# Candidate sums of a two-layer bidirectional GRU kept in the accumulator bank, with zeroings and output sigmoids in another place

## What is computed

```python
def step(hprev, gxt):
    gh = hprev @ whh.T + bhh
    r = jax.nn.sigmoid(gxt[:, :h] + gh[:, :h])
    z = jax.nn.sigmoid(gxt[:, h:2 * h] + gh[:, h:2 * h])
    n = jnp.tanh(gxt[:, 2 * h:] + r * gh[:, 2 * h:])
    hn = (1.0 - z) * n + z * hprev
    return (hn, hn)
...
fwd = _bigru(x_inner, ...)
bwd = jnp.flip(_bigru(jnp.flip(x_inner, 1), ...), 1)
y = jax.nn.silu(fwd + bwd) * jax.nn.silu(z)
```

## Time and profile before

| | |
|---|---|
| median of three runs | 1040.92 us |
| the profiled execution | 1043.19 us, its span 1041.2 us |
| the two loops (L2, L3) | 387.5 us each, 775 us of the span |
| busy in the span | PE 937.9 us (90%), DVE 831.3 (80%), ACT 746.7 (72%) |

### The profile page before, as it was taken

How to read it: one execution, slowest core, us unless ns; L and a number is a source line. 1 busy time by engine, 2 the same in 40 slices (tenths; PEclk the granted TensorE clock), 3 DMA queues, 4 the chain that set the end, 5 groups by cost and what they waited for, 6 DMA issues and landing times. The chain is left out here.

```text
span 1041.2 us, 54627 instructions
## 1 busy us (share of the span) xinstructions
PE 937.9 (90%) x22226; PEld 839.5 (81%) x22226; DVE 831.3 (80%) x4987; ACT 746.7 (72%) x4622; POOL 47.3 (5%) x24
## 2 busy tenths in 40 slices
PE   5678797799999999999999879999999999999997
PEld 3644785488988888888888747989888988888886
DVE  7753348688888888999999776888888899999993
ACT  4424571688888888888888528888887888888882
POOL 2001241100000000000000030000000000000000
PEclk9587899755555555555555557555555555555555
DMA  5020500000000000000000000000000000000001
GB/s 144 3 26 5 141 14 6 1 5 4 4 4 4 4 5 4 4 4 4 4 4 4 3 6 3 4 4 4 4 4 4 4 4 5 4 5 4 4 4 31
DMA packets 15000, 13.07 MB, mean 13 GB/s; under 512 B 12372, under 2 KB 13909, under 8 KB 14461
## 3 DMA queue, kind: packets, MB, share of 16 engines
q1 hardware_dynamic: 14749, 9.58, 3.8%
HBM read 8.74 MB, written 0.83 MB: 9 GB/s over the span
## 5 line engine op out<-in xcount | busy, mean ns | idle before, releaser
L1285 PE MATMUL L3s_cand_sum<-L_states,L_w_hidden 97*128 97x8 bf16 x2048 | 171.2, 174 | 0.0
L1285 PE MATMUL L2s_cand_sum<-L_states,L_w_hidden 97*128 97x8 bf16 x2048 | 171.2, 174 | 0.0
L1285 PE MATMUL L2s_reset_sum<-L_states,L_w_hidden 97*128 97x8 bf16 x2048 | 142.1, 180 | 2.5 <-DVE L_states L1147 1.7
L1285 PE MATMUL L3s_reset_sum<-L_states,L_w_hidden 97*128 97x8 bf16 x2048 | 142.1, 180 | 2.4 <-DVE L_states L1147 1.7
L1147 DVE TENSOR_TENSOR_SCAN L_states<-L3s_renew,L3s_terms 96x32 f32<-96x32 f32 x512 | 113.0, 221 | 23.0
L1147 DVE TENSOR_TENSOR_SCAN L_states<-L2s_renew,L2s_terms 96x32 f32<-96x32 f32 x512 | 113.0, 221 | 23.0
L1285 PE MATMUL L3s_keep_sum<-L_states,L_w_hidden 97*128 97x8 bf16 x2048 | 130.0, 174 | 0.0
L1285 PE MATMUL L2s_keep_sum<-L_states,L_w_hidden 97*128 97x8 bf16 x2048 | 130.0, 174 | 0.0
L1285 PEld LDWEIGHTS L3s_cand_sum<-L_states,L_w_hidden 97*128 97x128 f16 x2048 | 128.5, 104 | 0.0
L1285 PEld LDWEIGHTS L2s_cand_sum<-L_states,L_w_hidden 97*128 97x128 f16 x2048 | 128.4, 104 | 0.0
L1285 PEld LDWEIGHTS L2s_reset_sum<-L_states,L_w_hidden 97*128 97x128 f16 x2048 | 105.6, 112 | 21.8 <-issue 2.2
(11 more groups left out here) (252 smaller groups left out, 3160.1 us busy)
## 6 DMA issues: line engine op xcount, KB each, us to landing
L_wih_raw<-in_L_wih SPq DMA_DIRECT2D x2, 1152.0 KB, 11.1
lagged<-in_L_w SPq DMA_DIRECT2D x1, 1296.0 KB, 8.4
L_w_hidden_raw<-in_L_whh SPq DMA_DIRECT2D x2, 576.0 KB
stream<-in_x SPq DMA_DIRECT2D x2, 384.0 KB, 3.8
out<-stream SPq DMA_DIRECT2D x4, 192.0 KB, 2.1
l_idft<-in_idft SPq DMA_DIRECT2D x1, 400.0 KB
rpe_lw<-in_rpe_lw SPq DMA_DIRECT2D x1, 384.0 KB
lagged<-coefs SPq DMA_DIRECT2D x16, 24.0 KB, 2.2
```

What stands on the lines that cost most here:

```text
L1285: return e.matmul(dst, weights.hidden[0:rows, wp, GATES * (2 * g + j) + gate, :], rhs, start=False, stop=False, skip_group_check=True)
```

## The change

Three things. First, `candidate` no longer writes an SBUF tile: the scan writes into the third or fourth quarter (by q's parity) of the same candidate bank whose first two quarters it reads, and the tanh reads it there. Second, every zeroing and every output sigmoid on ScalarE now stands directly behind a reset sigmoid, through a new function `between`: a group's reset half behind its own reset sigmoid at s = 0, the other group's keep half behind the reset sigmoid at s = 1. Before, group 0's zeroings and all output sigmoids stood behind the tanh, and group 1's zeroings behind group 0's reset sigmoid of the step after. Third, TensorE's waits follow: the wait for the zeroed keep half moves to the hidden keep products, a step earlier in the count for group 1, and group 0's six keep input products are shared over five steps (s = 3 to 7) in place of six.

```diff
-        cand = pairs("cand", [C, 2, PER, 2])
...
+        cand = lambda g, q: cand_bank[g][q // STEPS % 2][0:C, 2 + q % 2].rearrange("p c s -> p (c s)")[:, 0:2 * PER]
...
-                    e.tensor_tensor_scan(flat(cand[g][:, x]), flat(reset[g][:, x]), flat(cand_sum(g, p)[0:C, :, :, s]), 0.0,
+                    e.tensor_tensor_scan(cand(g, q), flat(reset[g][:, x]), flat(cand_sum(g, p)[0:C, :, :, s]), 0.0,
                                          ALU.mult, ALU.add).then_inc(cand_ready[g], 1)
...
-                def zero(g, q):
-                    p, s = q // STEPS % 2, q % STEPS
-                    if 1 <= q // STEPS < CHUNK_COUNT - 1:
+                def zero(g, q, sums):
+
+                    e.activation(sums(g, 1 - q // STEPS % 2)[0:C], zeros[:], ACT.Copy).then_inc(zeroed[g], 1)
+
+                def between(g, q):
+
+                    chunk, s = divmod(q, STEPS)
+                    if 1 <= chunk < CHUNK_COUNT - 1:
                         if s == RESET_ZEROED:
-                            e.activation(reset_sum(g, 1 - p)[0:C], zeros[:], ACT.Copy).then_inc(zeroed[g], 1)
+                            zero(g, q, reset_sum)
                         if s == KEEP_ZEROED:
-                            e.activation(keep_sum(g, 1 - p)[0:C], zeros[:], ACT.Copy).then_inc(zeroed[g], 1)
+                            zero(1 - g, q, keep_sum)
+                    if q >= SEQ // 2 + STEPS and 4 <= 2 * s + g < 8:
+                        sigmoid_of_y(q - s - STEPS, 2 * s + g - 4)
...
-                        if g == 0 and q >= 1:
-                            zero(1, q - 1)
+                        between(g, q)
                         e.wait_ge(keep_summed[g], q + 1)
...
-                        e.activation(terms[g][:, x, :, 0], cand[g][:, x, :, 1], ACT.Tanh).then_inc(advanced[g], 1)
-                        if g == 0:
-                            zero(0, q)
-                        if q >= SEQ // 2 + STEPS and 4 <= 2 * s + g < 8:
-                            sigmoid_of_y(q - s - STEPS, 2 * s + g - 4)
+                        e.activation(terms[g][:, x, :, 0], cand(g, q)[:, 1::2], ACT.Tanh).then_inc(advanced[g], 1)
...
-                        before, at = divmod(q - 1, STEPS)
                         if q >= 1:
                             e.wait_ge(advanced[g], 5 * q)
-                        if 1 <= before < CHUNK_COUNT - 1 and at in (RESET_ZEROED, KEEP_ZEROED):
-                            e.wait_ge(zeroed[g], 2 * (before - 1) + (1 if at == RESET_ZEROED else 2))
+                        chunk = q // STEPS
+                        clearing = 1 <= chunk < CHUNK_COUNT - 1
+                        if clearing and s == RESET_ZEROED + 1:
+                            e.wait_ge(zeroed[g], 2 * (chunk - 1) + 1)
                         ahead(RESET, RESET_ZEROED + 1)
-                        ahead(KEEP, KEEP_ZEROED + 1)
+                        ahead(KEEP, KEEP_ZEROED + 2 - g)
...
+                        if clearing and s == KEEP_ZEROED + 1 - g:
+                            e.wait_ge(zeroed[g], 2 * (chunk - 1) + 2)
                         for j in range(2):
                             add(KEEP, 0, 0, j)
                             add(KEEP, 1, 0, j)
```

## The result

The changed kernel took 1011.47 us in the median of four runs (1010.84 to 1015.95), against 1040.68 (1040.25 to 1045.58) for the kernel before beside it: a ratio of 0.972, with a 95% interval from 0.968 to 0.976. It is 29 us faster; 38 were forecast. Run again it took 1015.17, ratio 0.972 (0.969 to 0.975).

The account below looks back on a forecast made before the run. Each 1.46 us step was taken as bound by a dependency ring through scan, tanh and new state. Terms -19.8 - 4.5 - 15.4 + 1.9 = -37.8 took 1040.9 to 1003 us; range 995 to 1022.

Parts of the forecast that it names:

- the dearer write: Rival: the scan's write to PSUM costs more, 46 ns giving 1023 us or the skill's figures 1030; chance 20%.
- the stall: Rival: TensorE's stall behind zeroings persists; half of 0.33 us per chunk staying gives 1013; 11% shared with tanh without gain.
- the idle tanh: Rival: the faster tanh saves nothing, in some steps (1008 us) or all (1018); 11% shared with the stall.
- Zeroings: First steps of each chunk: TensorE's 0.33 us stall behind a zeroing wholly removed, -19.8 us.
- output sigmoids: Second-half chunks: placed behind a reset sigmoid they cost nothing, saving 0.15 us per chunk, -4.5 us.
- TensorE: Group 0's turns: one more per chunk with three input products, costing 0.03 us each, +1.9 us.
- The tanh: Every group-step: reading PSUM makes it 37 ns shorter, counted as 0.03 us x 512, -15.4 us.
- the cap: New state also waits for the kept product, so only 30 to 40 ns per step can be saved on the tanh branch.
- the tanh gives nothing: Rival: VectorE's 96x64 operation before new state withholds 5.4 us (1008), or all 15.4 go (1018); 11% shared with the stall.
- The scan: Candidate scan on VectorE: writing to PSUM instead of SBUF taken to cost 0.
- The same-bank rival: Scan reading and writing one bank takes up to 0.21 us longer, giving 1106 us; slower or break-even by the write: 7%.
- What would show it: Signs if right: chunks of 11.44 plus 0.03 to 0.06 us, no zeroing waits, tanh near 181 ns, scan near 207.

Follow-up runs that it names:

- e1_places: Changed kernel with the candidate back in its SBUF tile, so only the places of zeroings and output sigmoids and group 0's keep shares differ from before: 1022.66 us, ratio 0.980.
- e4_extra_g1: Changed kernel with one more, unused input product on TensorE in every turn of group 1: 1017.04 us in one run, loop 371.83 us.
- e5_extra_g0: Changed kernel with one more, unused input product on TensorE in every turn of group 0: 1034.25 us in one run, loop 380.17 us.
- e3_two_inputs: Changed kernel with group 0's candidate input products in group 1's turn and its keep products shared 1, 2, 1, 1, 1: 1008.27 us, ratio 0.966.
- e7_own_first: As e3_two_inputs, but at s = 0 group 0's candidate input product stays in its own turn: 1009.10 us, ratio 0.967.

## Why the prediction was right, and which term was off

The sign, the mechanism and the range held (1011.5 in 995 to 1022); the forecast was 8 us too low. That the range held is in part luck: 1011.5 lies outside the 997 to 1009 in which the sum was said to hold, and among the numbers of the dearer write (1009 to 1030) and of the stall or the idle tanh (1010 to 1018). Neither the write nor the stall cost what these bands were drawn for; the largest share of the 8 us comes from the second ring, which no rival names.

*Zeroings, output sigmoids, TensorE.* Their terms were -19.8, -4.5 and +1.9, together -22.4; e1_places gives -22.3 in the loops. That the two agree so closely is luck: by the chunks of e1_places (11.733 and 11.732 against 12.019 and 12.194), zeroings and TensorE together gave 30 x 2 x 0.286 = 17.2 where 17.9 were forecast, the output sigmoids 15 x 2 x 0.176 = 5.3 where 4.5 were. No run separates the zeroings' places from the moved waits and group 0's shares. The rest, 7.7 of the 30.0 us that both loops lost, is left for the PSUM edit.

*The tanh, the term that failed: 15.4 forecast, 7.7 measured.* The 37 ns and the cap were right for a step; the count of 512 was wrong. Chunk by chunk, in one order (the causes overlap, and another order shares them out otherwise):

- The turns with three input products. The text took 0.03 for one such turn as something added to any step. It is a ring of its own, 1.466 long, that the tanh has no part in. With the 1.46 of before it was almost hidden; with 1.43 it shows in four of eight steps, which keep their length while the others shrink. Cost: 2 x 3.50 us with the short tanh, of which 2 x 1.45 were there with the long one: 4.1 us. e4_extra_g1, e5_extra_g0 and e3_two_inputs are the evidence: nothing for work in group 1's turns, 0.036 and 0.053 per turn for work in group 0's, and the long steps gone without three.
- VectorE's output operation in the second half. With e3_two_inputs a second-half chunk is 0.073 longer, with the long tanh 0.004: 15 x 2 x 0.069 = 2.1 us. This was the rival "the tanh gives nothing"; it was right in the place, but what it withheld was 0.012 of the 0.03 in each of the six steps.
- A step without either shrank by 0.027 (1.431 against 1.458 in e1_places), not 0.030: 1.5 us.

That is the whole of the missing 7.7. Step by step, from e1_places to the changed kernel, the shares are others: the 248 steps with three input products saved 0.006 each, 6.0 us less than forecast; the 90 others with an output operation 0.016 each, 1.3 less; the remaining ones 0.027, 0.5 less. In both orders the second ring is the largest share.

A hint of it stood in the earlier trace rows: the step from s = 5 to 6, which ends with a turn of three input products, was 1.49 long against 1.46, and a step longer than its neighbours is held by something that the neighbours are not. It was a weak hint: the turn at s = 7 had three input products too, and its step, from 332.89 in the earlier trace rows to this row of the same time line, took 1.46:

```profile
334.35 0.18 ACT L1224 ACTIVATE L2s_reset<-L2s_reset_sum 96x16 f32<-96x16 f32 x1
```

Had the saving been withheld from the four such turns of 31 chunks, 264 of 512 steps would have been left, 7.9 us. That this meets the 7.7 is luck in part: it leaves out the 1.5 us that those turns did save and the 1.8 that the others fell short by.

*The scan.* Forecast 0. Its mean is 205 ns in e1_places and 221 here; but it also starts earlier behind its reset sigmoid, and its end lies 0.439 behind that start against 0.431 (group 0, mean). So the write to PSUM costs 8 ns on the path: 36 - 8 = 28, and a step gained 27. The kept branch would have allowed 29, so the cap was in the right place too. The same-bank rival (up to 210 ns) and the dearer write (46 ns) are out. The Trainium skill ("Perfetto Trace Analysis", section "Optimizing Scalar/DVE Operations") has 65 ns more for DVE on PSUM than on SBUF, and 42 less for ScalarE: the trace agrees for ScalarE (36) and not for VectorE (8 to 16).

*The stall stays.* It did not: no wait for a zeroing is left, and the keep sigmoid is 0.28 behind its reset sigmoid. The first user of the cleared keep half is not the hidden keep product, as the prediction has it: that one waits, but it writes the other half, and the first input product goes to the cleared half a step later.

*What would show it.* Chunks of 11.47 to 11.50 were named and 11.60 came, 11.63 in the second half: the sign of the two causes above.

**The fastest version** is e3_two_inputs, with e7_own_first equal to it: ratio 0.966 (0.964 to 0.969), its loops 18.5 us shorter than before and 3.5 shorter than the change's. Open: why the steps of e7_own_first grew by some ns.

## What to carry to other kernels

A loop over engines holds several rings at once, and a saving in one counts only in the steps which that ring sets: list the steps that are already longer than the rest, find what holds them, and take them out of the count before multiplying. In-order engines make such rings between groups that share no data: here a scan of one group queued ahead of the other group's `h_lo` on VectorE, and TensorE's row of products closed it. To find which engine's work is on the ring, add one useless instruction to each turn of one group and then of the other: 0 us against 8 us per loop said it at once.

## What the hardware showed that was not expected

- VectorE's instructions with two SBUF inputs took up to twice as long while GpSimd ran elementwise work on SBUF (0.17 to 0.34 us; mean 0.28), and one with an input in PSUM did not (0.21). The Trainium skill ("SBUF — State Buffer", section "Who interferes with whom") says it so: two SBUF inputs contend with a GpSimd instruction that reads SBUF, one does not. By that rule and these rows the scan that reads PSUM was the only one spared.
- A scan that reads one PSUM bank and writes the same one ends 8 ns later on the path than when it writes SBUF (its mean is 16 ns longer).
- Outside the loops one code took 265.8 to 271.9 us, with the granted clock of the first 100 us at 0.83 in the shortest and 0.74 in another. Inside the loops, at 0.50 throughout, executions agreed to 0.04 us.
